# A graph layer on one core: the mix steps in 49 blocks in a row instead of two in each three blocks

## The reference

```
xn = layernorm(x)
support = xn @ weight
gnn = segment_sum(edge_weight[:, None] * support[dst], src)
# mix: q, k, v from xn; elu + 1; sums over all nodes, so no row is done before all k and v are
kv = einsum(k, v); z = 1 / (q . ksum + eps); t = q . kv * z
x1 = layer_norm(t + xn, ln1_g, ln1_b)
y  = gelu(x1 @ W1.T + b1) @ W2.T + b2
mix = layer_norm(y + x1, ln2_g, ln2_b)
x = x + gnn + mix
# then top-k of a score over all rows, an MLP on those rows, and x = x + result
```

## Time and profile before

| | us |
|---|---|
| median of 3 runs | 3671.97 (3671.89 to 3687.26) |
| the profiled execution | 3643.18 |
| its span | 3641.4 |
| attention blocks 2 to 47 | from 600.7 to 1197.2 |
| the loop with mix steps, blocks 52 to 117 | from 1265.3 to 2143.6 |
| blocks 118 to 127 | from 2143.6 to 2263 |

### The profile page before, as it was taken

One profiled execution on the slowest core, in us unless ns is written; L12 is line 12 of the kernel. 1 busy time (PEld: TensorE's weight loads), 2 busy tenths in 40 slices (PEclk: granted clock), 3 DMA queues, 4 the chain that ended last, 5 costly groups with the idle time before them and its releaser, 6 DMA issues.

```text
span 3641.4 us, 82338 instructions
## 1 busy us (share of the span) xinstructions
PE 3008.8 (83%) x18718; PEld 2284.4 (63%) x18718; DVE 2457.8 (67%) x6616; ACT 1620.0 (44%) x4142; POOL 2036.7 (56%) x2303
## 2 busy tenths in 40 slices
PE   3777757989999778878888885999999999349998
PEld 2444425666666666666666664777777777238887
DVE  7888894444444577677767773999999999862111
ACT  4444413555555444444444443444444444662332
POOL 1444443555555556655656665777777777313433
PEclk7889978999999899899999997999999999759999
DMA  5777735888888777766776776888888888651111
GB/s 169 249 249 249 261 122 188 277 269 276 277 272 274 252 230 228 230 226 225 238 226 223 228 234 219 273 279 276 277 276 276 278 274 275 231 185 52 53 53 43
DMA packets 427483, 818.34 MB, mean 225 GB/s; under 512 B 45499, under 2 KB 203191, under 8 KB 427256
## 3 DMA queue, kind: packets, MB, share of 16 engines
q1 hardware_dynamic: 348376, 559.80, 50.4%
q0 software_dynamic: 78880, 256.49, 18.6%
HBM read 459.96 MB, written 356.17 MB: 224 GB/s over the span
## 4 chain that ended last, share of the span: by engine, by line
PE 43%; POOL 15%; issue 12%; DVE 12%; ACT 6%; POOLq 4%; another core or an unknown queue 3%; DMA 3%; SPq 2%; DVEq 0%; ACTq 0%
POOL acc L738 15%; PE ps L958 15%; PE ps L1145 5%; PE ps L1135 5%; PE ps L971 5%; PE ps L967 2%; POOLq L735 2%; DVE acc L1513 2%; PE ps L1005 2%; ACT rowbuf L1271 2%; PE ps L1014 1%; DMA acc<-bucket_rows 1%; PE ps L929 1%; PE ps L979 1%
## 5 line engine op out<-in xcount | busy, mean ns | idle before, releaser
L706 POOL DMA_INDIRECT sorted_rows<-rowbuf,posu x896 | 925.6, 1033 | 766.4 <-ACT rowbuf L1271 506.9
L958 PE MATMUL ps<-mainbuf 128*128 128x256 bf16 x5376 | 740.3, 283 | 168.1 <-ACT rowbuf L1271 106.1
L1092 PE MATMUL ps<-rowbuf,mainbuf 128*128 128x256 f32 x3584 | 845.7, 393 | 24.2 <-DVE mainbuf L1890 19.4
L1271 ACT ACTIVATE rowbuf<-ps 128x512 f32<-128x512 f32 x896 | 514.6, 593 | 769.6 <-PE ps L958 408.1
L1890 DVE TENSOR_SCALAR mainbuf<-cols,rowbuf 128x128 f32<-128x128 f32 x1792 | 819.2, 526 | 43.6 <-DMA rowbuf<-sorted_rows 34.7
L738 POOL TENSOR_TENSOR acc<-acc,node 128x256 f32 x896 | 673.8, 752 | 196.1 <-POOL acc L738 130.2
L1092 PEld LDWEIGHTS ps<-rowbuf,mainbuf 128*128 128x128 f32 x3584 | 620.0, 189 | 249.8 <-DVE mainbuf L1890 179.6
L958 PEld LDWEIGHTS ps<-mainbuf 128*128 128x128 bf16 x5376 | 510.7, 101 | 305.3 <-ACT rowbuf L1271 154.9
L1365 ACT ACTIVATE node<-ps 128x512 f32<-128x512 f32 x448 | 267.5, 597 | 493.4 <-PE ps L1092 405.0
L1707 DVE TENSOR_SCALAR mainbuf<-mainbuf,lane 128x1024 bf16<-128x1024 bf16 (+1 forms) x256 | 116.4, 455 | 269.1 <-PE ps L958 206.2
L1340 ACT ACTIVATE rowbuf<-ps,fb_c 128x256 f32<-128x256 f32 x200 | 94.8, 474 | 254.1 <-PE ps L1135 252.5
(11 more groups left out here) (354 smaller groups left out, 4702.5 us busy)
## 6 DMA issues: line engine op xcount, KB each, us to landing
rowbuf<-sorted_rows SPq DMA_DIRECT2D x448, 516.0 KB, 4.5
mainbuf<-slot_rows_in_window SPq DMA_DIRECT2D x128, 448.0 KB
acc<-bucket_rows SPq DMA_DIRECT2D x128, 416.0 KB, 6.1
sorted_rows<-node SPq DMA_DIRECT2D x105, 258.0 KB, 2.4
mainbuf<-support_rows SPq DMA_DIRECT2D x128, 192.0 KB
sorted_rows<-rowbuf,posu POOLq DMA_INDIRECT x896
node<-in_x SPq DMA_DIRECT2D x104, 128.0 KB, 5.1
sorted_rows<-rowbuf SPq DMA_DIRECT2D x14, 903.0 KB, 4.9
```

The lines of the kernel that those rows point to most:

```text
L706: g.indirect_dma_start(pairs_d, bass.IndirectOffsetOnAxis(posu[:, PC * k + c:PC * k + c + 1], 0), rowbuf[:, S * k + 2 * c:S * k + 2 * c + ...
L958: last = mm(ps[:, MSG + (k + c) % 2, u * C:(u + 1) * C], oht[:, s * P:(s + 1) * P], win[:, k, v * C:(v + 1) * C], start=v == 0, stop=v == 2)
L1092: last = mm(ps[:, GRP + k, h * C:(h + 1) * C], ohw[:, k % 2, s * P:(s + 1) * P], rowbuf[:, BT * k + s, 0:C], start=t == 0, stop=t == 1)
L1271: A(rowbuf[:, S * k + 2 * c:S * k + 2 * c + 2, 0:C], ps[:, MSG + (k + c) % 2, :].rearrange("p (t c) -> p t c", t=2), ACT.Copy).then_inc(ro ...
```

## The change

The loop with mix steps has two blocks a turn instead of six, both with a mix step, and 22 turns instead of 11. It covers blocks 52 to 95 with mix steps 3 to 46, as many mix steps as before. Blocks 96 to 99 finish the mixing, and blocks 100 to 127 are plain. They are written out by the `while` loop below, as blocks 118 to 127 were. The step functions of the engines are the same.

```
--- before.py
+++ after.py
@@ -362,21 +362,15 @@
             step(h0, 1, mix=0, front=True)
             step(h0 + 1, 0, mix=1, front=True, mid=True)
             step(h0 + 1, 1, mix=2, front=True, mid=True, back=True)
-            turns = (NA - 5) // 4
+            turns = (NA - 4) // 2
             with eng.Fori(0, turns) as g:
                 if chain is not None:
-                    chain.enter(g, 4 * mixed)
-                m = 4 * g + 3
-                for r in range(6):
-                    h, k = 3 * g + h0 + 2 + r // 2, r % 2
-                    if r % 3 == 2:
-                        step(h, k)
-                    else:
-                        step(h, k, mix=m, front=True, mid=True, back=True)
-                        m = m + 1
+                    chain.enter(g, 2 * mixed)
+                for k in range(2):
+                    step(g + h0 + 2, k, mix=2 * g + 3 + k, front=True, mid=True, back=True)
             if chain is not None:
                 chain.leave(turns)
-            b, m = 2 * (h0 + 2) + 6 * turns, 4 * turns + 3
+            b, m = 2 * (h0 + 2) + 2 * turns, 2 * turns + 3
             while b < NSB:
                 if m < NA + 2:
                     step(b // 2, b % 2, mix=m, front=m < NA, mid=m <= NA, back=True)
```

## The result

The changed kernel is slower. Its median is 3706.14 us (3702.9 to 3706.99, 4 runs) against 3671.93 us (3671.83 to 3687.26) in the same comparison; the ratio is 1.0081, 95% interval [1.0061, 1.0101]. The forecast was 3649.5 us, in 3616 to 3690, so the time lies outside the range and on the other side of no change. On two further chips the ratio was 1.0114 [1.0086, 1.0142] and 1.0193 [1.0174, 1.0212].

What follows compares the result with a forecast made beforehand. VectorE was taken to bound mix blocks, GpSimd plain blocks. The terms 593.1 - 878.3 - 0.9 + 263.6 = -22.5 us, applied to the 3671.97 us median, gave 3649.5 us, range 3616 to 3690.

Steps and rivals of the forecast that it cites:

- Removed loop and run of plain blocks: Mixing part: the 66-block loop goes, 878.3 us; 22 more plain blocks at the end add 22 x 11.98 = 263.6 us.
- Drain blocks: Four blocks finishing the mixing, 51.5 us: the first now follows a mix block, 0.9 us less.
- Mix blocks: New mixing loop: 44 mix blocks in a row at 13.48 us, as in blocks 51 to 53, 593.1 us.
- (b): Mixing loop: a two-block body stays in place, avoiding the six-block body's 3.4 us stall a turn; no extra term.
- VectorE absorbs part of the 3.4 us: First block of a loop turn: VectorE hides part of GpSimd's 3.4 us stall; no separate size.
- collisions: Rival, mix blocks: GpSimd's addition and VectorE stretch each other; 14.28 us each, +12.7, 3684.7 us; chance 0.16 including lost smoothing.
- GpSimd falls behind: Rival, mix run: GpSimd's round outlasts VectorE's 13.5 us; 15.1 us a block, +48.8, time 3720.8 us; chance 0.14.
- the prediction's sign for this: Mix run: if the forecast holds, no eviction waits for "remote" as long as 5 us.
- Better mix run: Rival, mix run: all blocks take 12.82 us, 564.1 us together, time 3607.7 to 3620.5 us; chance 0.18.
- Reason (a), the smoothing: Old mix, mix, plain pattern: smoothing between block kinds gains less than it costs; VectorE's L1700 waits 53.4 us in 66 blocks.

Runs made afterwards that it cites:

- no_if: The changed kernel with GpSimd's never-taken general path for wide supports and its branch left out in all blocks: 3623.19 us, ratio 0.993.
- pad224_c: The changed kernel with 224 idle semaphore increments ahead of GpSimd's mixing loop, on a chip with 13.0 us attention blocks: 3696.11 us, ratio 1.0133.
- pad64_c: The changed kernel with 64 idle semaphore increments ahead of GpSimd's mixing loop, on a chip with 13.0 us attention blocks: 3619.12 us, ratio 0.9927.
- pad64: The changed kernel with 64 idle semaphore increments ahead of GpSimd's mixing loop, first run: 3626.46 us, ratio 0.9938.
- lots 1 and 3: Two groups of follow-up runs, each on one chip beside the kernel before; attention blocks took 13.0 us there.
- lot 2: A group of follow-up runs on one chip beside the kernel before; attention blocks took 11.7 us there, and the unchanged changed kernel had ratio 1.0193.
- pad64_no_add: The changed kernel with 64 idle increments ahead of GpSimd's mixing loop and GpSimd's bias addition left out of each mix step: ratio 1.0079.
- again_after: The changed kernel itself, unchanged, run again on another chip: 3538.26 us against 3472.37 us for the kernel before, ratio 1.0193.

## Why the prediction was wrong

**Removed loop and run of plain blocks: right.** 22 x 11.98 = 263.6 us was measured as 11.98 each for blocks 104 to 125 (2003.33 is the start of block 101, 2303.62 that of block 126: 300.29 us for 25, 12.01). That it fits to the hundredth is luck: the same blocks took 11.37 to 11.74 us in the later traces of this order on such chips. And the reason given for it was not right. I read GpSimd's 2.84 us ahead of a block's first scatter as a handover that bounds the block. The trace of after shows stops at skipped bodies in it, and no_if took them all away and won nothing. What bounds these blocks is open. TensorE's granted clock is 0.79 to 0.81 there with the stops and without, and 305 of the 907 matmuls of the expansion took 400 ns or more in no_if, against 11 of 1938 in its attention blocks; that makes the clock a candidate, which no run took away.

**Drain blocks: small miss.** 52.5 us instead of 50.6, +1.9. Block 52 started 9.9 us later than in the first trace of before, in a part that the change doesn't touch.

**Mix blocks: the step that failed, +74.8 us.** The term 44 x 13.48 = 593.1 was right for a run of mix blocks in which GpSimd doesn't stop: 13.59, 13.75 and 13.60 us in the three padded runs, and 13.61 without the branch. It failed at the sentence under (b), "two of them should stay in place as there". The term put the turn at nothing, because a sample of straight code had none in it. I compared the numbers of matmuls, which are TensorE's instructions. The engine that had shown the stall in block 64 was GpSimd, and its body should have been counted. By my count of the compiled program the attention loop on GpSimd is 318 instructions and the new mixing loop 324 (the traces show those that run, 56 and 62 a turn): nearly the same size, so even the right count would have pointed to "stays". What differs is where they lie. The padding shows it: moved by 0 places the loop stops, by 64 it doesn't, by 224 it does. The Trainium skill ("Runtime: NRT & Kernel Launch", Instruction fetch mechanics) says that instructions are held in pages of 256, two at a time, and that a taken branch to outside of the two waits for a fetch. An estimate by that rule, from the page's 256 and my own counts: 324 instructions fit if the loop begins at most 188 places into a page, and a begin between 230 and 255 places into one fits all three paddings, and the attention loop too, which by my count begins 742 instructions ahead. The trace agrees with the wait for a fetch: a packet of the instruction queue lies in each of the 42 stops of the mix run. The runs agree with the rule at these three places of the loop; the place in the page itself isn't seen in any trace. In the plain blocks, though, the same code stops on one chip and not on another, and so which skipped bodies stop is open. I had that rule on the table and used it for the six-block body alone, and as a gain.

**The second half of the same step: a branch that skips.** I charged the stall to turns only. In the trace of before, 10 of 66 skipped bodies had it already, and by the counts above the compiled body of `If(wide > 0)` is 131 of the 159 instructions of a step in a loop. A branch over instructions that are never run is a taken branch too. The two branches of a turn stand 3.7 us apart in the records above, on an engine with all seven scatters of that block still to issue.

**"VectorE absorbs part of the 3.4 us": half of it.** Two stops of some 3 us for each turn of two blocks are 6 us; the turn became 3.1 us longer (2 x (15.16 - 13.60)). In VectorE's account half of that is waiting and the other half the stretch of the rival "collisions", but only 0.09 us a block (0.56 - 0.47) needs the two together. The late addition meets other instructions: that of L1771 is over 1.2 us in 8 of 44 blocks in after (L1765 there) and in none in pad224_c (mean 712 ns), against 21 in pad64_c (1280), and the Newton instructions take its place, where 0.16 us becomes 1.98. The stretch isn't all or nothing either, as the prediction had it: in pad64 that instruction also took 1.05, 1.40 and 1.47 us.

**The rivals.** "GpSimd falls behind" had the price, 15.1 us a block, within 0.1 of the 15.18 measured, and the sign, with a chance of 0.14. Its mechanism was another: I had worked it out as a round of seven issues, an addition and a handover that is full. GpSimd is busy 375.6 of 667.9 us (56%), and in pad64_c 373.1 of 598.3. It isn't full, it stands still at two branches. Seventeen of the 308 evictions in the mix run stood behind a wait of over 5 us, the prediction's sign for this; in pad64 none did. What I offered against it, 65% busy over blocks 51 to 53, had no say: those blocks lie in straight code and hold no turn. "Better mix run" (12.8) would have needed the addition gone.

**Reason (a), the smoothing**, counted for nothing that I can show: lots 1 and 3 put the two orders within some 2 us of each other once GpSimd doesn't stop in the mixing part (with VectorE's stops still in the old one). On the chip of lot 2 the order itself costs: 28 us in pad64_no_add, which has neither stops in the mix run nor the addition. No padded kernel with the addition ran there; with 13.00 + 0.47 for a mix block the stops of again_after would be worth 44 x 0.4 = 18 us of the 66, and some 1.4% would be left to the order. That is an estimate, and its cause is open.

## What to carry over

- Count a loop body on each engine, in that engine's own instructions, bodies of untaken branches included, and look at the instruction queue of the window: 3 packets or 100 in 600 us tells at once whether a loop stays in place (38 to 40 where only VectorE's does not). A sample taken from straight code (blocks 51 to 53 here) has no turn in it and is no price for a loop.
- Where a two-block loop costs 1.5 us a block more than its straight copy, try some padding ahead of it before anything else, or take rarely used paths out of the body (a second copy of the stream behind one branch at its head).
- A row that names an engine as the releaser of a long idle time is to be held against the end of that engine's instruction; here it ended 4 us before. The sequencer's records name the stop.

## What the runs showed of the hardware

- Behind a branch of a loop or over a skipped body on GpSimd or VectorE the next record comes either within some 0.4 us or after some 3 (nine in ten of 523 stops lie between 2.2 and 5.0 us), and in all 42 stops of the changed kernel's mix run an 8 KB packet of the instruction queue falls into the gap. Where the loop lies decides it: 160 more idle instructions ahead of the loop (224 against 64) made the kernel 77 us (2.1%) slower. In the plain blocks nearly every skip stopped on the other chips and none (of 25) on the chip of lot 2, in the same program.
- With the stops came a lower granted clock of TensorE (0.93 to 0.95 for the mix run, against 1.00) on the chips where a mix block lost 1.5 us, and none (1.00) on the chip of lot 2.
- A GpSimd addition of [128 x 512] float32 (1.27 us) stretches a VectorE instruction beside it: 0.16 became 1.98, ending within 0.03 us of the addition, and 0.69 became 1.90, ending 0.6 us behind it. Without it the 44 mix blocks took 577.6 us instead of 598.3.
- On the chip of lot 1 GpSimd's stops cost nothing in the plain blocks (11.54 us with them, 11.67 without).
- The same attention block took 13.0 us in four of the comparisons and 11.7 on the chip of lot 2, with the granted clock at 0.99 to 1.00 on both; the changed kernel's ratio went from 1.008 and 1.011 to 1.019 with it. Why is open.
